# A causal mask carried in the score operands, and late keys scored for late queries only, in a decoder layer on one core

## The reference, cut to what matters

```python
q = (einsum('bld,ed->ble', x, Wq) + bq) ...        # 16 heads of 16 dims; k and v alike
scores = einsum('bhqd,bhkd->bhqk', q, k) * 0.25
bias = where(q_pos >= k_pos, -slope[h] * abs(q_pos - k_pos), -inf)
out = einsum('bhqk,bhkd->bhqd', softmax(scores + bias), v)
x = x + (out @ Wo.T + bo)                          # self-attention
x = x + cross_attention(layernorm(x), ctx)         # 16 heads, 120 keys, no mask
x = x + tanh(((layernorm(x) @ W0) @ W1) @ W2 + bias)
```

## Time and profile before

| | us |
|---|---|
| median of 3 runs | 2563.94 (2559.92 to 2565.83) |
| the profiled execution | 2562.27 |
| its span, first to last instruction | 2560.4 |

### The profile page before, as it was taken

The page is one execution under the profiler, slowest core; times in us unless marked ns, Lnnn a source line. Parts: engine busy times, 40 slices in busy tenths (PEclk is TensorE's granted clock), DMA queues, the critical chain, the costliest instruction groups (busy, mean ns, idle before and its releaser), DMA issues.

```text
span 2560.4 us, 70719 instructions
## 1 busy us (share of the span) xinstructions
PE 2422.5 (95%) x23737; PEld 1982.0 (77%) x23864; DVE 1706.9 (67%) x3714; ACT 1401.3 (55%) x3067; POOL 716.9 (28%) x1359
## 2 busy tenths in 40 slices
PE   3799999999999999999999999999999999999995
PEld 2578778878878878887887887887888788788773
DVE  3476676676677677677667667767767766766752
ACT  2355555555655555555555565555555555556552
POOL 2122322322332332322232233233232223223311
PEclk8899999999999999999999999999999999999996
DMA  2334334334333433333333333343333343333320
GB/s 74 80 95 106 89 92 105 98 92 105 100 85 99 110 91 103 101 85 97 105 97 92 105 100 85 99 110 91 101 102 84 98 105 97 93 105 99 87 76 21
DMA packets 162893, 240.69 MB, mean 94 GB/s; under 512 B 21792, under 2 KB 86032, under 8 KB 159768
## 3 DMA queue, kind: packets, MB, share of 16 engines
q1 hardware_dynamic: 161308, 240.02, 35.4%
q10 hardware_dynamic: 1536, 0.01, 0.0%
HBM read 53.12 MB, written 33.55 MB: 34 GB/s over the span
## 4 chain that ended last, share of the span: by engine, by line
PE 80%; DMA 5%; ACT 4%; DVE 4%; issue 3%; SPq 2%; ACTq 1%; POOL 1%; DVEq 0%; POOLq 0%
PE ps_misc L491 15%; PE ps_misc L477 9%; PE ps_score L575 6%; PE ps_attend L603 6%; PE ps_misc L633 5%; DMA q_stack<-neg_max_t_s 5%; PE ps_score L577 5%; PE ps_score L579 5%; PE ps_max L556 4%; PE ps_max L543 4%; PE ps_score L588 4%; PE ps_max L533 3%; PE ps_misc L648 3%; PE ps_misc L461 2%; PE ps_max L539 2%
## 5 line engine op out<-in xcount | busy, mean ns | idle before, releaser
L753 ACT ACTIVATE probs<-ps_score 128x384 f32<-128x384 f32 x1024 | 468.6, 493 | 134.8 <-PE ps_score L579 129.3
L904 DVE TENSOR_REDUCE neg_max_s<-ps_max 128x2 f32<-128x512 f32 (+1 forms) x768 | 482.7, 681 | 41.3 <-PE ps_max L543 32.6
L760 ACT ACTIVATE xprobs<-ps_score 120x512 f32<-120x512 f32 x512 | 295.5, 599 | 236.5 <-PE ps_score L588 229.2
L1021 POOL TENSOR_SCALAR ve_LN<-mv_LN 128x2 f32<-128x2 f32 x192 | 37.0, 193 | 1259.9 <-DVE mv_LN L926 1259.9
L577 PE MATMUL ps_score<-q_stack,k_stack 128*128 128x256 f32 x1024 | 373.4, 365 | 0.0
L912 DVE TENSOR_REDUCE neg_max_x<-ps_max 128x4 f32<-128x480 f32 x512 | 313.8, 649 | 63.5 <-PE ps_max L556 63.5
L575 PE MATMUL ps_score<-mask_k,ident_b 128*128 128x256 bf16 x1024 | 287.5, 281 | 24.1 <-DMA q_stack<-neg_max_t_s 19.0
L579 PE MATMUL ps_score<-q_stack,k_stack 128*128 128x256 f32 x1024 | 287.5, 281 | 0.0
L588 PE MATMUL ps_score<-xq_stack,xk_stack 128*120 128x256 f32 x1024 | 227.7, 315 | 3.5 <-DMA xq_stack<-neg_max_t_x 2.8
L1047 POOL TENSOR_TENSOR res<-res,chain_n 128x512 f32<-128x512 f32 x64 | 82.5, 1289 | 456.0 <-ACT chain_n L798 456.0
L577 PEld LDWEIGHTS ps_score<-q_stack,k_stack 128*128 128x128 f32 x1024 | 203.2, 198 | 1.4
(11 more groups left out here) (153 smaller groups left out, 5847.9 us busy)
## 6 DMA issues: line engine op xcount, KB each, us to landing
k_stack<-k_nat SPq DMA_DIRECT2D x192, 256.0 KB, 3.6
q_stack<-q_nat SPq DMA_DIRECT2D x192, 256.0 KB, 3.6
xq_stack<-q_nat SPq DMA_DIRECT2D x192, 256.0 KB, 3.7
xk_stack<-scr_xk SPq DMA_DIRECT2D x192, 128.0 KB, 2.9
x_in<-in_x SPq DMA_DIRECT2D x64, 256.0 KB, 2.8
scr_xk<-k_nat SPq DMA_DIRECT2D x32, 512.0 KB, 3.5
out_y<-res SPq DMA_DIRECT2D x64, 256.0 KB, 2.2
ctx_in<-in_ctx SPq DMA_DIRECT2D x32, 240.0 KB, 4.2
```

The costliest lines, as they stand in the source:

```text
L753: act.activation(probs[:, h % 8, :], bank_of("SCORE", i, b, h)[:, P:4 * P], ACT.Exp)\
L760: act.activation(xprobs[0:C, at:at + 2, :], blocks(bank_of("XSCORE", i, b, u))[0:C], ACT.Exp).then_inc(sem("xprobs_ready"), 1)
L904: dve.tensor_reduce(o, ins, AX.X, ALU.max, negate=True).then_inc(sem("max_taken"), 1)
```

## The change

**Mask rows.** `AUG` moves to rows 7 and 15. Rows 2, 3, 5 and 6 of every eight, 64 rows in all, get constants. GpSimd makes `steps_q` and `steps_k`, 64 rows by 256 tokens; row r stands for tokens 4r to 4r+3. A query has a positive power of two in its own row only. A key has -2^70 in every row of an earlier four tokens, so that each query of those fours sees it masked, and inside its own four a value that grows with its place, so that the product is at least 8192 below zero where the key is later than the query and at most 2^-25 where it isn't. SP writes them into the four stacks with 16 DMAs of 16 rows x 16 heads x 256 tokens, each row's 1 KB read once per head. The constants are 32-bit powers of two, so the 16-bit view that MAX uses holds them too. The mask matmuls and `ident_b`, `mask_q`, `mask_k` are gone.

**Late keys.** In SCORE the matmul of the late keys runs over the late queries alone, 128 moving columns instead of 256.

```diff
-AUG = 2
+AUG = (7, 15)
+STEPS = (2, 3, 5, 6)
+NSTEP = 4
+UP = [2.0 ** (57 - 38 * p) for p in range(NSTEP)]
+DOWN = [0.0] + [-2.0 ** (38 * p - 82) for p in range(1, NSTEP)]
+BEYOND = -2.0 ** 70
...
             sp.wait_ge(sem("rows_set"), 16 * 7)
+            sp.wait_ge(sem("steps_cut"), 2)
+            for p in range(2):
+                for stacks, made in ((q_stack, steps_q), (k_stack, steps_k)):
+                    for n, row in enumerate(STEPS):
+                        sp.dma_start(stacks[p][row:P:ROWSTEP, :, :].bitcast(F32),
+                                     made[n::NSTEP, :].unsqueeze(1).to_broadcast([P // ROWSTEP, H, T]))\
+                            .then_inc(sem("steps_set"), 16)
...
-                        pe.wait_ge(sem("rows_set"), 16 * 7)
+                        pe.wait_ge(sem("steps_set"), 16 * 16)
...
-                    pe.matmul(bk[:, :], ident_b[:, :], mask_q[:, :, :].rearrange("p a b -> p (a b)"),
-                              start=True, stop=False, skip_group_check=True)
...
-                    pe.matmul(two[:, :, P:T], ident_b[:, :], mask_q[:, 0:2, :],
-                              start=True, stop=False, skip_group_check=True)
...
-                pe.matmul(bk[:, P:3 * P], ident_b[:, :], mask_k[:, :, :].rearrange("p a b -> p (a b)"),
-                          start=True, stop=False, skip_group_check=True)
-                pe.matmul(bk[:, 0:T], ks[:, h, P:T], qs[:, h, :], start=False, stop=False,
-                          skip_group_check=True)
-                pe.matmul(bk[:, T:2 * T], ks[:, h, 0:P], qs[:, h, :], start=False, stop=True,
-                          skip_group_check=True).then_inc(sem("scores_ready"), 1)
+                pe.matmul(bk[:, P:T], ks[:, h, P:T], qs[:, h, P:T], start=True, stop=True)
+                pe.matmul(bk[:, T:2 * T], ks[:, h, 0:P], qs[:, h, :], start=True, stop=True)\
+                    .then_inc(sem("scores_ready"), 1)
```

More of the change, by code:

```diff
@@ L354, in _ @@
             for p in range(2):
-                sp.dma_start(q_stack[p][AUG:AUG + 2, :, :].bitcast(F32), ones).then_inc(sem("rows_set"), 16)
+                sp.dma_start(q_stack[p][AUG[0]:AUG[1] + 1:AUG[1] - AUG[0], :, :].bitcast(F32), ones)\
+                    .then_inc(sem("rows_set"), 16)
                 sp.dma_start(k_stack[p][SHIFT:SHIFT + 1, :, :].bitcast(F32), ones[0:1]).then_inc(sem("rows_set"), 16)
@@ L431, in _ @@
         def _(pe):
-            pe.wait_ge(sem("consts"), 4)
+            pe.wait_ge(sem("consts"), 1)
             pe.wait_ge(sem("w_loaded"), 16 * (len(PREP) + 1))
@@ L543, in maxima @@
                         mm = pe.matmul(two[:, j, :], narrow(qs[0:SHIFT, h, P:T]),
-                                       narrow(ks[0:SHIFT, h, :]), start=False, stop=(j == 1),
-                                       skip_group_check=True)
+                                       narrow(ks[0:SHIFT, h, :]), start=True, stop=True)
                 mm.then_inc(sem("max_ready"), 1)
@@ L992, in _ @@
             pool.memset(ident[:, :], 0.0).then_inc(sem("const0"), 1)
-            pool.memset(ident_b[:, :], 0.0).then_inc(sem("const0"), 1)
-            pool.memset(mask_q[:, :, :], 0.0).then_inc(sem("const0"), 1)
-            pool.memset(mask_k[:, :, :], 0.0).then_inc(sem("const0"), 1)
-            pool.wait_ge(sem("const0"), 4)
-            for m in (ident, ident_b):
-                pool.affine_select(out=m[:, :], in_=m[:, :], compare_op=ALU.not_equal, fill=1.0, base=0,
-                                   pattern=[[-1, P]], channel_multiplier=1).then_inc(sem("consts"), 1)
-            pool.affine_select(out=mask_q[:, :, :], in_=mask_q[:, :, :], compare_op=ALU.is_ge, fill=BIG,
-                               base=0, pattern=[[0, 4], [-1, P]], channel_multiplier=1)\
-                .then_inc(sem("consts"), 1)
-            pool.affine_select(out=mask_k[:, :, :], in_=mask_k[:, :, :], compare_op=ALU.is_ge, fill=BIG,
-                               base=0, pattern=[[0, 2], [1, P]], channel_multiplier=-1)\
-                .then_inc(sem("consts"), 1)
+            pool.wait_ge(sem("const0"), 1)
+            pool.affine_select(out=ident[:, :], in_=ident[:, :], compare_op=ALU.not_equal, fill=1.0, base=0,
+                               pattern=[[-1, P]], channel_multiplier=1).then_inc(sem("consts"), 1)
+            for p in range(NSTEP):
+                pool.memset(steps_q[:, p::NSTEP], UP[p]).then_inc(sem("steps_laid"), 1)
+                pool.memset(steps_k[:, p::NSTEP], DOWN[p]).then_inc(sem("steps_laid"), 1)
+            pool.wait_ge(sem("steps_laid"), 2 * NSTEP)
+            for tile in (steps_q, steps_k):
+                pool.affine_select(out=tile[:, :], in_=tile[:, :], compare_op=ALU.is_ge, fill=0.0, base=0,
+                                   pattern=[[1, T]], channel_multiplier=-NSTEP).then_inc(sem("steps_from"), 1)
+            pool.wait_ge(sem("steps_from"), 2)
+            for tile, beyond in ((steps_q, 0.0), (steps_k, BEYOND)):
+                pool.affine_select(out=tile[:, :], in_=tile[:, :], compare_op=ALU.is_ge, fill=beyond,
+                                   base=NSTEP - 1, pattern=[[-1, T]], channel_multiplier=NSTEP)\
+                    .then_inc(sem("steps_cut"), 1)
             pool.memset(k_stack[1][:, :, :].bitcast(F32), 0.0)
```

15 lines of the change are left out of this document (6 added, 9 removed).

## The result

| | before | after |
|---|---|---|
| median, us | 2564.89 (4 runs) | 2527.32 (2526.46 to 2531.2, 4 runs) |
| ratio | | 0.9859 (0.9841 to 0.9877) |
| span of the profiled execution, us | 2560.4 | 2525.1 |

What follows compares the result with a forecast made beforehand. PE was busy 95% of the span but only 80% of the last chain, with DVE full in the maxima. Collecting 1.65 us per step, 62 x 1.65 = 102, less 9 at the start, gave 93 us less: 2470 us, range 2425 to 2520.

Steps and rivals of the forecast that it cites:

- The loads hide: Rival, SCORE: 32-bit load ready under a 128-column matmul, head 0.175 us, 28 us more gained, 2442 us; chance 0.14.
- the clock stays at its upper level: Against a slower rival: PE's longer waits drop its clock to 1.2 GHz, two slowed blocks per step give 2657 us; chance 0.03.
- part 1, the work of the scores: SCORE on PE: a head falls from 0.36 to 0.235 us, 16 x 0.125 = 2.0 us less PE work per step.
- the stage of the scores, what is collected: Of 2.0 us PE work saved in SCORE, 1.4 us shortens odd steps and 0.9 us even ones; waits swallow the rest.
- the scores don't collect: Rival: exponentials gate PE at more places or the 128-column matmul costs full 0.12 us; 2517 us, chance 0.17.
- the stage of the maxima: From last XMAX to SCORE 0: of 1.8 us mask work removed per step, 0.5 us collected; 0.4 at LN2_T.
- part 3, the start: Before the first input load: 16 more DMAs, 4.19 MB, delay the first statistics by 6 to 11.5 us, taken as 9.
- both of my bounds: DMA rate at the start: weight loads 277 to 326 GB/s, stack copies 216 to 220, giving 13.7 or 19 us.

Runs made afterwards that it cites:

- all late keys: Changed kernel with the late keys scored for all 256 queries again, still without the mask matmul: 2527.48 us, ratio 0.986 to the kernel before.
- short exponentials: Changed kernel with each head's exponential on ACT over 128 instead of 384 columns, the rest keeping old values: 2519.24 us, ratio 0.984 to the kernel before.

## Why the prediction was wrong, point by point

**Right.** The price of a head in a stream of long matmuls: 0.06 + 0.17 where 0.057 + 0.06 + 0.12 was forecast. "The loads hide" falls with it, and the clock stays at its upper level in the steady part. The experiment with all late keys fits the reason given: the pair takes 0.24 us with 128 moving columns less or more, so its columns don't set its time, and its two 32-bit loads are what is left. The Trainium skill ("TensorE: Matmul & The Clock Gate", section "LDWEIGHTS (loading the stationary operand)") puts a load at columns / 1.2 ns, from which 0.21 us is an estimate for two loads; the trace has 0.23. The gain up to MAX_T was 0.49 for a forecast 0.5, with DVE's pause nearly closed. Even steps gained less than odd ones, by 0.4 for a forecast 0.5. Only half of that is the forecast place: in even steps the stretch from ATTEND 1 to LN3_T, with SCORE 13 in it, grew from 1.52 to 1.75 us with the change, while in odd steps it fell to 1.42, and a buffer of its own for XK gives even steps 0.48 and odd ones nothing. The other half was not forecast and lies at LN2_T (below), so that the difference came out so near is in part luck.

**Wrong 1, part 1, the work of the scores: 16 x 0.125.** I priced a head behind long matmuls and used that for all sixteen. Behind ATTEND the saving is 0.03, of which the mask is 0.02 (shown by the mask put back there), at SCORE 0 it is 0.03, behind the cross maxima 0.06. So PE's work fell by 1.5 us, not 2.0. The rows on an exposed load were in my hands; I applied them to the new matmul and not to what the mask had covered.

**Wrong 2, the stage of the scores, what is collected: 1.4 and 0.9.** Measured are 0.43 and 0.22. In both kinds of step 0.5 of the miss is the work that was never saved (Wrong 1). In odd steps the other 0.4 is waits: the new ones sum to 1.0 us, where I had 0.6 (0.25 at SCORE 2, 0.1 at SCORE 8 and 11, 0.25 at LN3_T). SCORE 2 is as forecast. SCORE 8 and 11 have 0.38 for the 0.1, and LN3_T only 0.13. What I didn't have at all is XHEADS_OUT 1 and XOUT_T, 0.23. I had taken what the first five heads save as collected but for SCORE 2; ATTEND 0 comes 0.03 earlier. From LN2_T on a chain of ACT, DVE and PE sets the pace there (XQ, its high part, its low part, XHEADS_OUT, XOUT_T). The experiment on XQ's low part shows that gate: with half of it left out ATTEND 0 comes 0.23 earlier, while taking away the wait at SCORE 2 alone moves nothing there. In even steps the waits sum to 1.2 us where I had 1.1 (0.25 at SCORE 2 and the 0.9 up to SCORE 13), so there the work is nearly the whole miss. This was the rival "the scores don't collect", whose 2517 came nearest. Its mechanism was half right: the exponentials do gate PE at more places, SCORE 8 and 11. But short exponentials gain only in even steps, since in odd ones XQ's low part and POOL's LN3 stand right behind them.

**Wrong 3, the stage of the maxima, even steps.** I let ACT evict LN2_T and then the maxima, and that holds: SCORE 0 starts 4.0 us behind LN2_T in both kinds of step, before and after. I collected 0.4 at LN2_T and 0.5 at the end of the stage. Odd steps collect 0.44. Even ones collect 0.26, since POOL's LN2 comes some 0.17 later there, already in the kernel before. I had read POOL's end from one odd step and used it for both kinds. The mean is 0.35 for 0.5. That PE would wait for POOL is right: 0.22 and 0.40 for a forecast 0.4 to 0.5.

**Wrong 4, part 3, the start: 9.** It was 13.2, outside the 6 to 11.5. The copies ran at 190 GB/s, below both of my bounds (216 and 326), and at that rate 4.19 MB take 22 us. The bounds came from copies with other shapes; each row's 1 KB is read again for every head here. That this repetition is what made them slower was not tested.

In the sum: (0.35 + 0.34) x 62 = 43 us in the full steps for 102, and some 6 more in the partial ones at the ends; less 14, it is the 35 of the span. The range was too narrow since all rivals with a good chance kept 0.95 us per step or more.

Still open is the reason behind the price of a pair: no run changed the loads alone, so that they set it is inferred from the runs with other columns and the other order.

## What to carry to other kernels

A matmul taken out of a stream gives back its distance to its neighbours only if it wasn't covering one of their weight loads; price it at each place where it stands, by its neighbour. Before counting a saved head as time, follow the chain that is not made of it (here XQ to XOUT_T) and see whether it is the one that the next stage waits for. Where steps alternate, read the slack in both kinds. A load that everything hangs on is issued ahead of setup copies, even if these are needed soon after.

## What the runs showed of the hardware that I had not expected

- A pair of matmuls with 32-bit operands and weights of 128 columns costs 0.23 to 0.24 us whether it has 256 + 256 or 128 + 256 moving columns (2527.48 and 2527.32 us for the kernel). With the longer first it is 0.18, and the next matmul with a 32-bit load costs up to 0.06 more; cross maxima with 16-bit weights cost no more behind it (2518.77 us).
- A bf16 matmul of 256 columns placed between outputs of 32 rows (ATTEND) and a 32-bit load costs 0.02 us, for 0.12 behind long matmuls.
- Sixteen DMAs of 256 KB each that repeat 1 KB rows took SP up to 5.01 / 4 = 1.25 us each to issue, with the DMA engines 97% busy at 190 GB/s; the load behind them took 1.25 to issue as well, for 0.41 ahead of them.
